# Last layer of a two-layer decoder: values and context table in one PSUM bank, three norms on ScalarE, a new order of the turn

## The chip, the cores and the metric

One core of a Trainium2 chip. The metric is the device time of one launch in microseconds (us). Engines are named as in the profile: PE (TensorE, matmul), DVE (VectorE), ACT (ScalarE), POOL (GpSimd), SP (SyncE, here only a DMA queue). SBUF is the working memory of 128 partitions, PSUM the eight banks that PE writes its results to; POOL reads and writes SBUF alone.

## What is computed

The reference applies six blocks to x of shape (2, 1024, 256), each as `x = layernorm(x + block(x))` with eps 1e-5 and no gain or bias. Layer 0 has a causal linear attention, a cross attention with quantised weights and a mixture of eight experts of which each token takes one. Layer 1, the last, is the part that the change is about:

```python
def attn1(x):                          # per token, 16 heads of 16
    Q, K, V = (heads(x @ W.T) for W in (W_Q, W_K, W_V))
    sK = softmax(swapaxes(K, -1, -2))          # softmax over the 16 numbers of each head of K
    tran_V = einsum('bldh,blhe->blde', sK, V)  # a 16 x 16 table for every token
    return einsum('blhd,blde->blhe', softmax(Q), tran_V)

def xattn1(x, ctx):                    # 16 heads of 64, 64 context rows in one frame
    xn = layernorm(x) * gamma + beta
    return softmax(q @ k.T * 64**-0.5 + mask) @ v @ Wo + bo

def ffn1(x):                           # 256 -> 1024 -> 1024 -> 1024 -> 256, ternary weights
    h = silu((x @ w1.T) * s1) * ((x @ w2.T) * s2)
    h = gelu((h @ h1.T) * sh1); h = gelu((h @ h2.T) * sh2)
    return (h @ w3.T) * s3

x = layernorm(x + attn1(x)); x = layernorm(x + xattn1(x, ctx)); x = layernorm(x + ffn1(x))
```

## The kernel before

The program runs its stages one after the other, each with its own instruction list per engine and semaphores between them. Two stages matter here.

**Experts** (`stage_experts`, L1457 on). 23 slots of 128 rows go through two matmul layers. SP's queue loads a slot's rows (`rows`, L1497, 128 KB) and its expert's first weights (`weights`, L1491, 1024 KB) into one of two buffers, `following` (L1501) waits until the buffer is free and loads both. Rows and weights of the first two slots are loaded by the stage before. At its start the queue waits for the copy of the last layer's weights to be complete, issues three loads for later (`wqkv1` of 768 KB, `w1` and a piece of 1024 KB each, L1508 to L1511), and then `following(2, 0)`. On PE, `turn_rows` (L1537) turns a slot's rows and `hidden` (L1544) and `output` do the matmuls; the third slot's rows are turned between the hidden layers of the first and the second.

**The last layer** (`stage_layer1`, L1685 on). Tokens are 16 tiles of 128, eight blocks i of both sequences b (k = 2i + b counts them). A tile has a long chain through the engines: moments of x (DVE), a power -0.5 (POOL, `power`), the normed x3 (DVE, L2205), its turning (PE, `turned_x3`) and copy (ACT, `x3_copied`), the projection (PE, `qkv`), softmaxes of Q and K (DVE and ACT), the 16 x 16 tables (`contexts`) and their product with Q (`attended`), the norm x4 and beside it xn for the cross attention (DVE, L2264), scores (PE), their maximum (DVE), 16 exponentials with sums (ACT, `score_exp`), probabilities (DVE), their turning (PE), `summed` (PE), the norm x5. Then both tiles of a block, a pair j of 256 tokens, go through the feed-forward part: `first` (eight units of two products), two `hidden` layers (eight units of 16 matmuls each) and `final`. All its operands are split in a high and a low part: ACT writes the high part, POOL subtracts for the low one (`gate_lower`, `lower_parts`).

DVE does the per-token tables by hand: `contexts` and `attended` (L2234, L2244) come in four quarters, each of two products of 128x512 and two reduces after them, written as

```python
products(..., lambda at, n: V.tensor_tensor(part[n], spread(kn[:, at:at + TWO, :], 2, DH),
                                            spread(vs[b][:, :, :], 1, TWO), ALU.mult),
         lambda at, n: V.tensor_reduce(to[:, at:at + TWO, :], part[n], AX.X, ALU.add))
```

The values `vs[b]` are an SBUF tile (it shares its place with `xT[b]`), filled from PSUM bank 3 by an ACT copy (`v_copied`, L2064). The table `T` is an SBUF tile too. The other half of bank 3 takes the turned x3.

The order of the work is written out by hand, once per engine, in a function `trip(n)` (L1831 POOL, L2004 PE, L2128 ACT, L2338 DVE): the trip of turn n does the start of block n, the attentions of block n - 1, the feed-forward part of block n - 2 and the last norm of block n - 3. `tile`, `pair` and `row_of` leave out what lies outside the eight blocks. A turn here is the time from one first `final` to the next. Each engine runs its list strictly in order, so an instruction that waits holds everything behind it; no planner moves anything.

Before the first trip, POOL issues 16 gathers of the experts' results (L1864 to L1872) with the first two `x_powered` between them, after the sixth and the twelfth gather. After the last `final`, the last norm `y_normed` (DVE, L2333) and a store of 128 KB per tile end the program.

## Time and profile before

| | us |
|---|---|
| median of 3 runs (1346.11 to 1347.29) | 1346.78 |
| the profiled execution, whole | 1346.4 |
| its span on the core | 1344.8 |
| PE busy in the span | 1073.1 (80%) |
| DVE busy | 936.4 (70%) |
| ACT busy | 591.8 (44%) |
| POOL busy | 359.6 (27%) |

Busy is the time in which an engine executes an instruction; waiting in a queue is not in it. The span runs from the first to the last instruction. The last layer takes a little over half of it, from 636 us to the end. The mean granted clock of PE over the span is 0.917 of full speed.

### The profile page before, as it was taken

The numbers are of one execution on the slowest core, as the hardware profiler recorded it, in microseconds if no ns is written. First come the engines' busy times: TensorE is split into PE (matmuls) and PEld (weight loads), VectorE is DVE, ScalarE is ACT, GpSimd is POOL, SyncE is SP. The second block draws the span as 40 slices with busy tenths as digits, with TensorE's granted clock in tenths as the row PEclk, the third lists the DMA queues.
The fourth block names the chain that finished last, engine by engine and source line by source line (L and its number), as shares of the span: only waits on it lengthen the run. The fifth ranks groups of instructions, "written<-read, shape, count | busy, mean of one in ns | idle before, by whom it ended". The sixth has DMA issues, their size and how long they took to land. (4 is left out here: it accounts for less than half of the span.)

```text
span 1344.8 us, 21004 instructions
## 1 busy us (share of the span) xinstructions
PE 1073.1 (80%) x6765; PEld 895.6 (67%) x6770; DVE 936.4 (70%) x1861; ACT 591.8 (44%) x1626; POOL 359.6 (27%) x494
## 2 busy tenths in 40 slices
PE   0589999766888599998344798889888898897887
PEld 0478888644366488887122687677767787786787
DVE  4689999765774022222599998989898998989231
ACT  0244444141263232232022556567566656747552
POOL 1001011100034200000400435436262633536232
PEclk9889999885896799999667799999999999999899
DMA  8015710002402566664440000000000000000000
GB/s 286 19 71 184 237 49 5 0 1 109 174 1 94 197 226 226 242 222 153 172 203 1 1 1 1 8 0 8 0 4 4 0 8 0 8 0 9 1 9 9
DMA packets 24263, 98.88 MB, mean 74 GB/s; under 512 B 3761, under 2 KB 15217, under 8 KB 17617
## 3 DMA queue, kind: packets, MB, share of 16 engines
q1 hardware_dynamic: 16368, 73.60, 14.8%
q10 hardware_dynamic: 5200, 17.37, 3.9%
q0 software_dynamic: 2640, 7.21, 1.6%
q8 instruction: 30, 0.49, 0.2%
q14 instruction: 25, 0.20, 0.1%
HBM read 87.96 MB, written 21.76 MB: 82 GB/s over the span
## 5 line engine op out<-in xcount | busy, mean ns | idle before, releaser
L1989 PE MATMUL bank<-n_hA_hi_reduced,ffn_h 128*128 128x256 f32 x512 | 126.8, 290 | 9.2 <-POOL n_hA_lo_reduced L1812 5.5
L1989 PE MATMUL bank<-n_hB_hi_reduced,ffn_h 128*128 128x256 f32 x512 | 129.9, 296 | 1.5 <-DVE n_hB_lo_reduced L2326 1.5
L1989 PE MATMUL bank<-n_hB_lo_reduced,ffn_h 128*128 128x256 f32 x512 | 125.4, 287 | 0.0
L1989 PE MATMUL bank<-n_hA_lo_reduced,ffn_h 128*128 128x256 f32 x512 | 123.8, 284 | 0.0
L1606 ACT ACTIVATE e_hT<-bank,e_b 128x128 f32<-128x128 f32 x184 | 52.4, 368 | 135.4 <-PE bank L1549 135.4
L1989 PEld LDWEIGHTS bank<-n_hA_hi_reduced,ffn_h 128*128 128x128 f32 x512 | 99.2, 194 | 11.0 <-POOL n_hA_lo_reduced L1812 10.2
L1989 PEld LDWEIGHTS bank<-n_hB_hi_reduced,ffn_h 128*128 128x128 f32 x512 | 101.1, 197 | 3.3 <-issue 3.3
L2240 DVE TENSOR_TENSOR d_prod<-d_qk,d_xT 128x512 f32<-128x512 f32 x128 | 102.6, 841 | 0.5
L1989 PEld LDWEIGHTS bank<-n_hB_lo_reduced,ffn_h 128*128 128x128 f32 x512 | 101.0, 197 | 1.7 <-issue 1.7
L1989 PEld LDWEIGHTS bank<-n_hA_lo_reduced,ffn_h 128*128 128x128 f32 x512 | 99.1, 194 | 0.2
L1631 DVE TENSOR_TENSOR e_y<-bank,e_b 128x256 f32<-128x256 f32 x23 | 9.8, 424 | 125.3 <-PE bank L1561 125.3
L2252 DVE TENSOR_TENSOR d_prod<-d_qk,d_T 128x512 f32<-128x512 f32 x128 | 92.4, 761 | 0.3
L1549 PE MATMUL bank<-e_xsT,e_w 128*128 128x128 f32 x736 | 88.3, 279 | 0.2 <-DVE e_xsT L1623 0.2
L1819 POOL TENSOR_TENSOR n_hA_lo_reduced<-n_hA_lo,n_hA_hi_reduced 128x256 fp32r<-128x256 f32 x60 | 55.3, 922 | 123.9 <-ACT n_hA_lo L2125 123.3
L1549 PEld LDWEIGHTS bank<-e_xsT,e_w 128*128 128x128 f32 x736 | 86.5, 196 | 0.6 <-DVE e_xsT L1623 0.6
L1561 PE MATMUL bank<-w2e,e_hT 128*128 x368 | 83.1, 379 | 0.0
L2242 DVE TENSOR_REDUCE d_T<-d_prod 128x32 f32<-128x512 f32 x128 | 81.2, 674 | 0.0
L2254 DVE TENSOR_REDUCE d_r<-d_prod 128x32 f32<-128x512 f32 x128 | 81.1, 673 | 0.0
L562 PE MATMUL bank<-a_prod_a,ident 128*128 128x160 f32 x512 | 75.5, 307 | 7.0 <-DVE a_prod_a L714 6.1
L1970 PE MATMUL bank<-d_x5T_hi_reduced,ffn_w 128*128 128x256 f32 x256 | 66.1, 298 | 16.7 <-ACT n_hB_lo L2105 9.1
L562 PEld LDWEIGHTS bank<-a_prod_a,ident 128*128 128x128 f32 x512 | 71.8, 194 | 10.8 <-DVE a_prod_a L714 10.7
L2084 ACT ACTIVATE d_pr<-bank,d_score_max 128x64 f32<-128x64 f32 x256 | 75.9, 349 | 2.2 <-DVE d_score_max L2277 2.0
(344 smaller groups left out, 2686.1 us busy)
## 6 DMA issues: line engine op xcount, KB each, us to landing
e_w<-in_W SPq DMA_DIRECT2D x23, 1024.0 KB, 5.2
ffn_weights<-in_F ACTq DMA_DIRECT2D x2, 5632.0 KB, 20.8
e_piece<-ffn_weights SPq DMA_DIRECT2D x11, 1024.0 KB, 4.8
ffn_h<-ffn_weights SPq DMA_DIRECT2D x2, 4096.0 KB, 18.8
w2e<-in_W SPq DMA_DIRECT2D x1, 4096.0 KB, 13.2
w2e<-in_W SPq DMA_DIRECT2D x2, 2048.0 KB, 16.6
ffn_w<-ffn_weights SPq DMA_DIRECT2D x3, 1024.0 KB, 7.4
expert_rows<-zero ACTq DMA_DIRECT2D x1, 2944.0 KB, 10.7
```

The source lines that it names most:

```text
L562: last = nc.tensor.matmul(bank_a[:, 0:PAIRS], m.ident[:, :], prod_a[:, d, :], start=(d == 0), stop=(d == DH - 1))
L1549: last = nc.tensor.matmul(bank_h[u][f // 4][:, f % 4 * P:(f % 4 + 1) * P], w1[u][:, k, f * P:(f + 1) * P], xsT[u][:, k, :], start=(k == 0) ...
L1561: last = nc.tensor.matmul(bank_y[u][:, 0:D], hT[u][:, k, :], m.w2e[:, bass.ds(e, 1), k, :], start=(k == 0), stop=(k == KF - 1))
L1606: last = nc.scalar.activation(hT[u][:, k, :], bank_h[u][k // 4][:, k % 4 * P:(k % 4 + 1) * P], ACT.Relu, bias=b1[:, bass.ds(e, 1), k])
L1819: nc.gpsimd.tensor_tensor(dst[1][1][:, f, :], dst[1][0][:, f, :], dst[0][1][:, f, :].bitcast(F32), ALU.subtract).then_inc(ready, 1)
L1970: last = nc.tensor.matmul(F[f % 2][:, n * PAIR:(n + 1) * PAIR], weight(w[:, k, f * P:(f + 1) * P], fast), operand(x5T[part][1][:, k, :, :] ...
L1989: last = nc.tensor.matmul(F[f % 2][:, 0:PAIR], weight(w[:, k, f * P:(f + 1) * P], fast), operand(src[part][1][:, k, :], fast), start=(c == ...
L2084: last = nc.scalar.activation(pr[:, h * SC:(h + 1) * SC], bank_s[h // 8][:, h % 8 * SC:(h % 8 + 1) * SC], ACT.Exp, bias=score_max[b][:, 1, ...
L2240: lambda at, n: V.tensor_tensor(part[n], spread(kn[:, at:at + TWO, :], 2, DH), spread(vs[b][:, :, :], 1, TWO), ALU.mult),
L2242: lambda at, n: V.tensor_reduce(to[:, at:at + TWO, :], part[n], AX.X, ALU.add))
L2252: lambda at, n: V.tensor_tensor(part[n], spread(qn[:, at:at + TWO, :], 2, DH), spread(T, 1, TWO), ALU.mult),
L2254: lambda at, n: V.tensor_reduce(heads[:, at:at + TWO, :], part[n], AX.X, ALU.add))
```

## The change

- **Bank.** `T` and the values become the two halves of bank 3, read by DVE where PE wrote them. `vs`, the ACT copies `v_copied` and the SBUF table go. The projection of the values is split from `qkv` into `projected_v` with a place of its own in PE's list; it waits for `v_read`, which DVE signals after the last quarter of `attended`. The turned x3 goes to the second half of bank 4.
- **Norms.** x3, x4 and the last norm are computed by ACT as rstd * x + (-mean * rstd) in one instruction; POOL makes the offset with two more products on [128x1] after its power. xn stays on DVE. `out_summed` on DVE now waits for x4 from ACT.
- **Order.** All four lists are reordered; ACT's last norms need a trip more at the end. POOL's first two `x_powered` come after four and eight gathers.
- **Experts.** The third rows' load is issued ahead of the three later loads, on `xs_turned` alone.

```diff
+sp.wait_ge(xs_turned, 1)
+rows(2, 0)
 sp.wait_ge(m.weights_copied, 32)
 sp.dma_start(m.wqkv1[:, :, :], ins["wqkv1"]).then_inc(m.early_loaded, 16)
 sp.dma_start(m.w1[:, :, :].rearrange("p k n -> p (k n)"), m.ffn[:, 0:2 * FF]).then_inc(m.early_loaded, 16)
 sp.dma_start(piece[:, :], m.ffn[:, 0:2 * FF]).then_inc(piece_loaded, 16)
-following(2, 0)
+sp.wait_ge(h_done, 2)
+weights(2, 0)
...
-vs = [t[:, :, :].rearrange("p k (e h) -> p (k e) h", h=H) for t in xT]
-T = late("d_T", [P, DH, DH], F32)[:, :, :]
...
+T = bank_v[:, D:2 * D].rearrange("p (e d) -> p e d", e=DH)
+values = bank_v[:, 0:D].rearrange("p (e h) -> p e h", h=H)
...
+def negated(st, to):
...
+    return nc.gpsimd.tensor_tensor(st[:, to:to + 1], st[:, 6:7], m.mhalf[:, 2:3], ALU.mult)
...
+def offset(st, rstd, to):
...
+    return nc.gpsimd.tensor_tensor(st[:, to:to + 1], st[:, to:to + 1], st[:, rstd:rstd + 1], ALU.mult)
...
 def attn_powered(k, i, b):
     g.wait_ge(q["attn_var"], k + 1)
-    nc.gpsimd.tensor_tensor(stats[b][:, 10:12], stats[b][:, 8:10], m.mhalf[:, :],
+    after("x4", k - 1)
+    nc.gpsimd.tensor_tensor(stats[b][:, 10:12], stats[b][:, 8:10], m.mhalf[:, 0:2],
                             ALU.pow).then_inc(q["attn_pow"], 1)
+    negated(stats[b], 12).then_inc(q["x4_less"], 1)
+    g.wait_ge(q["attn_pow"], k + 1)
+    g.wait_ge(q["x4_less"], k + 1)
+    offset(stats[b], 10, 12).then_inc(q["x4_offset"], 1)
...
 def x_powered(k, i, b):
     powered(k, "x", xstats[b])
+    after("x3", k - 1)
+    negated(xstats[b], 10).then_inc(q["x_less"], 1)
+    g.wait_ge(q["x_pow"], k + 1)
+    g.wait_ge(q["x_less"], k + 1)
+    offset(xstats[b], 9, 10).then_inc(q["x_offset"], 1)
...
 def y_powered(j, b):
     g.wait_ge(y_var, 2 * j + b + 1)
     power(nc, m, ystats[b]).then_inc(y_pow, 1)
+    negated(ystats[b], 10).then_inc(y_less, 1)
+    g.wait_ge(y_pow, 2 * j + b + 1)
+    g.wait_ge(y_less, 2 * j + b + 1)
+    offset(ystats[b], 9, 10).then_inc(y_offset, 1)
...
 def trip(n):
     if not (isinstance(n, int) and n < 2):
         tile(x_powered, n, 0)
+    pair(lower_parts, n - 3, 1, 4, 8)
+    tile(out_powered, n - 2, 1)
     tile(attn_powered, n - 1, 0)
     if isinstance(n, int) and n == 1:
         x_powered(2, 1, 0)
-    pair(gated_product, n - 2, 0, 2)
+    tile(x5_kept, n - 2, 1)
+    row_of(added, n - 3, 0)
+    row_of(added, n - 3, 1)
+    pair(gated_product, n - 2, 0, 4)
     pair(gate_lower, n - 2, 0, 1)
-    pair(gated_product, n - 2, 2, 4)
-    pair(gate_lower, n - 2, 1, 2)
-    pair(gated_product, n - 2, 4, 5)
-    pair(gate_lower, n - 2, 2, 3)
-    pair(gated_product, n - 2, 5, 8)
+    pair(gated_product, n - 2, 4, 6)
+    pair(gate_lower, n - 2, 1, 3)
+    pair(gated_product, n - 2, 6, 8)
     pair(gate_lower, n - 2, 3, 8)
-    row_of(added, n - 3, 1)
     row_of(y_powered, n - 3, 0)
-    pair(lower_parts, n - 2, 0, 0, 2)
     row_of(y_powered, n - 3, 1)
-    pair(lower_parts, n - 2, 0, 2, 5)
-    tile(attn_powered, n - 1, 1)
     if not (isinstance(n, int) and n == 0):
         tile(x_powered, n, 1)
-    pair(lower_parts, n - 2, 0, 5, 8)
+    pair(lower_parts, n - 2, 0, 0, 6)
+    tile(attn_powered, n - 1, 1)
+    pair(lower_parts, n - 2, 0, 6, 8)
     tile(out_powered, n - 1, 0)
+    pair(lower_parts, n - 2, 1, 0, 2)
     tile(x5_kept, n - 1, 0)
-    pair(lower_parts, n - 2, 1, 0, 8)
-    tile(out_powered, n - 1, 1)
-    tile(x5_kept, n - 1, 1)
-    row_of(added, n - 2, 0)
+    pair(lower_parts, n - 2, 1, 2, 4)
...
     g.wait_ge(m.y_stored[u], 16 * ((NS + 1 - u) // 2))
 for t in range(TB):
-    if t == 3:
+    if t == 2:
         x_powered(0, 0, 0)
-    elif t == 6:
+    elif t == 4:
         x_powered(1, 0, 1)
...
 def turned_x3(k, i, b):
     pe.wait_ge(q["x3"], k + 1)
-    after("v_copied", k)
+    after("x3T", k)
+    after("out_var", k - 2)
     for c in range(KD):
-        last = nc.tensor.transpose(bank_v[:, D + c * P:D + (c + 1) * P], x3[b][:, c * P:(c + 1) * P],
+        last = nc.tensor.transpose(bank_o[:, D + c * P:D + (c + 1) * P], x3[b][:, c * P:(c + 1) * P],
                                    m.ident[:, :])
     last.then_inc(q["x3_turned"], 1)
...
 def qkv(k, i, b):
     pe.wait_ge(q["x3T"], k + 1)
     after("pre", k)
-    for lo, hi, to in ((0, 2 * D, bank_qk), (2 * D, 3 * D, bank_v)):
-        for c in range(KD):
-            last = nc.tensor.matmul(to[:, 0:hi - lo], xT[b][:, c, :], m.wqkv1[:, c, lo:hi],
-                                    start=(c == 0), stop=(c == KD - 1))
+    for c in range(KD):
+        last = nc.tensor.matmul(bank_qk[:, 0:2 * D], xT[b][:, c, :], m.wqkv1[:, c, 0:2 * D],
+                                start=(c == 0), stop=(c == KD - 1))
     last.then_inc(q["qkv_done"], 1)
+def projected_v(k, i, b):
+    pe.wait_ge(q["x3T"], k + 1)
+    after("v_read", k)
+    for c in range(KD):
+        last = nc.tensor.matmul(bank_v[:, 0:D], xT[b][:, c, :], m.wqkv1[:, c, 2 * D:3 * D],
+                                start=(c == 0), stop=(c == KD - 1))
+    last.then_inc(q["v_done"], 1)
...
 def summed(k, i, b):
     pe.wait_ge(q["probT"], k + 1)
     after("out_var", k)
+    pe.wait_ge(q["x3T"], min(k + 3, NT) if isinstance(k, int) else k + 3)
...
@@ -2007,25 +2046,30 @@
     tile(qkv, n, 0)
     pair(hidden, n - 2, 0, 0, 2, fast)
     tile(turned_probs, n - 1, 0)
-    pair(hidden, n - 2, 0, 2, 7, fast)
+    pair(hidden, n - 2, 0, 2, 6, fast)
     tile(summed, n - 1, 0)
+    pair(hidden, n - 2, 0, 6, 7, fast)
+    tile(projected_v, n, 0)
     tile(turned_xn, n - 1, 1)
     pair(hidden, n - 2, 0, 7, 8, fast)
+    tile(scores, n - 1, 1)
+    pair(hidden, n - 2, 1, 0, 1, fast)
     tile(turned_x3, n, 1)
-    tile(scores, n - 1, 1)
-    pair(hidden, n - 2, 1, 0, 3, fast)
+    pair(hidden, n - 2, 1, 1, 2, fast)
+    tile(qkv, n, 1)
+    pair(hidden, n - 2, 1, 2, 4, fast)
     tile(turned_x5, n - 1, 0)
-    pair(hidden, n - 2, 1, 3, 5, fast)
-    tile(qkv, n, 1)
     tile(turned_probs, n - 1, 1)
-    pair(hidden, n - 2, 1, 5, 8, fast)
+    pair(hidden, n - 2, 1, 4, 8, fast)
     tile(summed, n - 1, 1)
     row_of(final, n - 2, 0, fast)
+    tile(turned_x5, n - 1, 1)
     row_of(final, n - 2, 1, fast)
-    tile(turned_x5, n - 1, 1)
-    pair(first, n - 1, 0, 4, fast)
+    pair(first, n - 1, 0, 1, fast)
+    tile(projected_v, n, 1)
+    pair(first, n - 1, 1, 2, fast)
     tile(turned_xn, n, 0)
-    pair(first, n - 1, 4, 8, fast)
+    pair(first, n - 1, 2, 8, fast)
     tile(scores, n, 0)
...
-def v_copied(k, i, b):
-    act.wait_ge(q["qkv_done"], k + 1)
-    nc.scalar.activation(vs[b][:, :, :].rearrange("p a b -> p (a b)"), bank_v[:, 0:D],
-                         ACT.Copy).then_inc(q["v_copied"], 1)
...
 def xn_copied(k, i, b):
     act.wait_ge(q["xn_turned"], k + 1)
+    act.wait_ge(q["v_done"], k + 1)
...
+def x3_normed(k, i, b):
+    act.wait_ge(q["x_offset"], k + 1)
+    after("xn_turned", k - 1)
+    nc.scalar.activation(x3[b][:, :].unsqueeze(1), m.x[:, row(i, b), :], ACT.Identity,
+                         bias=xstats[b][:, 10:11], scale=xstats[b][:, 9:10]).then_inc(q["x3"], 1)
+def x4_normed(k, i, b):
+    act.wait_ge(q["x4_offset"], k + 1)
+    after("out_var", k - 1)
+    nc.scalar.activation(x4[b][:, :], r[b][:, :], ACT.Identity, bias=stats[b][:, 12:13],
+                         scale=stats[b][:, 10:11]).then_inc(q["x4"], 1)
+def y_normed(j, b):
+    act.wait_ge(y_offset, 2 * j + b + 1)
+    nc.scalar.activation(m.x[:, row(j, b), :], m.x[:, row(j, b), :], ACT.Identity,
+                         bias=ystats[b][:, 10:11], scale=ystats[b][:, 9:10]).then_inc(y_ready, 1)
 def trip(n):
+    tile(x3_normed, n, 0)
+    pair(gate_upper, n - 2, 5, 6)
     tile(x3_copied, n, 0)
-    pair(gate_upper, n - 2, 7, 8)
+    pair(gate_upper, n - 2, 6, 8)
     tile(score_exp, n - 1, 0)
-    pair(hidden, n - 2, 0, 0, 5)
+    pair(hidden, n - 2, 0, 0, 1)
+    row_of(y_normed, n - 3, 0)
+    row_of(y_normed, n - 3, 1)
+    pair(hidden, n - 2, 0, 1, 2)
     tile(probs_copied, n - 1, 0)
-    pair(hidden, n - 2, 0, 5, 7)
+    pair(hidden, n - 2, 0, 2, 4)
+    tile(x4_normed, n - 1, 0)
+    pair(hidden, n - 2, 0, 4, 6)
     tile(qk_exp, n, 0)
+    tile(x3_normed, n, 1)
     tile(xn_copied, n - 1, 1)
-    pair(hidden, n - 2, 0, 7, 8)
-    tile(v_copied, n, 0)
+    pair(hidden, n - 2, 0, 6, 8)
     pair(hidden, n - 2, 1, 0, 1)
     tile(x3_copied, n, 1)
-    pair(hidden, n - 2, 1, 1, 3)
+    pair(hidden, n - 2, 1, 1, 2)
     tile(score_exp, n - 1, 1)
-    pair(hidden, n - 2, 1, 3, 4)
+    pair(hidden, n - 2, 1, 2, 4)
     tile(x5_copied, n - 1, 0)
-    tile(v_copied, n, 1)
-    pair(hidden, n - 2, 1, 4, 6)
     tile(probs_copied, n - 1, 1)
-    pair(hidden, n - 2, 1, 6, 8)
+    tile(x4_normed, n - 1, 1)
+    pair(hidden, n - 2, 1, 4, 8)
+    tile(qk_exp, n, 1)
     tile(x5_copied, n - 1, 1)
-    tile(qk_exp, n, 1)
-    pair(first, n - 1, 0, 2)
+    pair(first, n - 1, 0, 4)
     pair(gate_upper, n - 1, 0, 1)
-    pair(first, n - 1, 2, 4)
-    pair(gate_upper, n - 1, 1, 2)
     pair(first, n - 1, 4, 6)
     tile(xn_copied, n, 0)
-    pair(gate_upper, n - 1, 2, 4)
+    pair(gate_upper, n - 1, 1, 4)
     pair(first, n - 1, 6, 8)
-    pair(gate_upper, n - 1, 4, 7)
-for n in range(2):
+    pair(gate_upper, n - 1, 4, 5)
+for n in range(3):
     trip(n)
-with act.Fori(0, TB - 2) as i:
-    trip(i + 2)
-for n in range(TB, TB + 2):
+with act.Fori(0, TB - 3) as i:
+    trip(i + 3)
+for n in range(TB, TB + 3):
...
-def x3_normed(k, i, b):
-    v.wait_ge(q["x_pow"], k + 1)
-    after("xn_turned", k - 1)
-    V.tensor_scalar(x3[b][:, :].unsqueeze(1), m.x[:, row(i, b), :], xstats[b][:, 6:7],
-                    xstats[b][:, 9:10], ALU.subtract, ALU.mult).then_inc(q["x3"], 1)
...
-    v.wait_ge(q["v_copied"], k + 1)
+    v.wait_ge(q["v_done"], k + 1)
...
              lambda at, n: V.tensor_tensor(part[n], spread(kn[:, at:at + TWO, :], 2, DH),
-                                           spread(vs[b][:, :, :], 1, TWO), ALU.mult),
+                                           spread(values, 1, TWO), ALU.mult),
...
+    if quarter == 3:
+        v.sem_inc(q["v_read"], 1)
...
-    link(V.tensor_scalar(x4[b][:, :], r[b][:, :], stats[b][:, 6:7], stats[b][:, 10:11], ALU.subtract,
-                         ALU.mult))
...
 def out_summed(k, i, b):
     v.wait_ge(q["out_done"], k + 1)
+    v.wait_ge(q["x4"], k + 1)
     link(V.tensor_tensor(r[b][:, :], bank_o[:, 0:D], x4[b][:, :], ALU.add))
...
-def y_normed(j, b):
-    v.wait_ge(y_pow, 2 * j + b + 1)
-    V.tensor_scalar(m.x[:, row(j, b), :], m.x[:, row(j, b), :], ystats[b][:, 6:7], ystats[b][:, 9:10],
-                    ALU.subtract, ALU.mult).then_inc(y_ready, 1)
...
 def trip(n):
     if not (isinstance(n, int) and n == 1):
         tile(x3_moments, n, 0)
-    tile(x3_normed, n - 1, 1)
+    tile(softmaxes, n - 1, 0)
+    tile(x4_and_xn, n - 2, 1)
+    tile(contexts, n - 1, 0, 0)
     tile(out_summed, n - 2, 0)
-    tile(softmaxes, n - 1, 0)
-    tile(contexts, n - 1, 0, 0)
-    tile(x5_normed, n - 2, 0)
+    tile(contexts, n - 1, 0, 1)
     tile(scores_max, n - 2, 1)
-    tile(contexts, n - 1, 0, 1)
     tile(contexts, n - 1, 0, 2)
     tile(contexts, n - 1, 0, 3)
+    tile(x5_normed, n - 2, 0)
+    tile(prepared, n - 1, 1)
     tile(probabilities, n - 2, 1)
     tile(attended, n - 1, 0, 0)
     tile(attended, n - 1, 0, 1)
-    tile(x5_split, n - 2, 0)
     tile(attended, n - 1, 0, 2)
     tile(attended, n - 1, 0, 3)
     tile(out_summed, n - 2, 1)
-    tile(prepared, n - 1, 1)
+    tile(x5_split, n - 2, 0)
     tile(x5_normed, n - 2, 1)
     if isinstance(n, int) and n == LAST + 3:
         last_lower_parts(0)
         last_lower_parts(1)
     row_of(sums_read, n - 3, 0)
+    tile(attention_summed, n - 1, 0)
+    tile(x5_split, n - 2, 1)
     row_of(sums_read, n - 3, 1)
-    tile(x5_split, n - 2, 1)
     if isinstance(n, int) and n == LAST + 2:
         last_gates()
-    tile(attention_summed, n - 1, 0)
-    row_of(y_moments, n - 3, 0)
     tile(softmaxes, n - 1, 1)
     tile(x4_and_xn, n - 1, 0)
     if isinstance(n, int) and n == 1:
         x3_moments(2, 1, 0)
+    row_of(y_moments, n - 3, 0)
     tile(contexts, n - 1, 1, 0)
+    row_of(y_moments, n - 3, 1)
     tile(contexts, n - 1, 1, 1)
     tile(contexts, n - 1, 1, 2)
-    tile(x3_normed, n, 0)
     tile(scores_max, n - 1, 0)
     tile(contexts, n - 1, 1, 3)
     tile(attended, n - 1, 1, 0)
+    tile(x3_moments, n, 1)
     tile(probabilities, n - 1, 0)
-    row_of(y_moments, n - 3, 1)
-    row_of(y_normed, n - 3, 0)
     tile(attended, n - 1, 1, 1)
-    row_of(y_normed, n - 3, 1)
     tile(attended, n - 1, 1, 2)
-    tile(x3_moments, n, 1)
+    tile(prepared, n, 0)
     tile(attended, n - 1, 1, 3)
     tile(attention_summed, n - 1, 1)
-    tile(prepared, n, 0)
-    tile(x4_and_xn, n - 1, 1)
...
-TRIP_LINKS = 108
+TRIP_LINKS = 106
```

(Twelve spaces of indentation are left out.) `TRIP_LINKS` counts the waits of DVE on itself in a trip.

## Rows read from the trace of the kernel before

**Rows 1.** Busy time by stage: from:to, length, PE, PEld, DVE, ACT, POOL, granted clock, DMA.

```profile
635.90:821.70 185.80, 112.44 (x530) 81.81 (x531) 156.62 (x296) 65.82 (x227) 54.79 (x65) 0.78 0.18 69
...
821.70:897.60 75.90, 65.99 (x449) 56.57 (x448) 68.95 (x128) 48.84 (x144) 35.98 (x44) 1.00 0.01 4
...
897.60:975.50 77.90, 67.94 (x451) 58.33 (x449) 71.00 (x130) 48.77 (x144) 35.63 (x44) 0.98 0.01 3
...
1207.20:1282.60 75.40, 63.54 (x430) 57.25 (x429) 44.06 (x83) 44.53 (x137) 33.20 (x42) 0.93 0.01 4
```

**Rows 2.** Groups of PE, five turns: busy us, mean ns, idle before by releaser.

```profile
L1928 PE MATMUL bank<-ident,d_pr 128*128 128x128 f32 x80 | 11.3, 285 | 16.4 <-DVE d_pr L2284 16.4
...
L1891 PE MATMUL bank<-ident,d_x 128*128 128x128 f32 x20 | 4.2, 294 | 14.2 <-ACT d_xT L2066 7.9 <-DVE d_x L2208 6.3
```

**Rows 3.** Groups of DVE over the same five turns, 821.7 to 1207.2 us.

```profile
L2240 DVE TENSOR_TENSOR d_prod<-d_qk,d_xT 128x512 f32<-128x512 f32 x80 | 66.3, 869 | 0.3
...
L2252 DVE TENSOR_TENSOR d_prod<-d_qk,d_T 128x512 f32<-128x512 f32 x80 | 59.4, 781 | 0.2
...
L2268 DVE TENSOR_SCALAR d_x<-d_r,d_stats 128x256 f32<-128x256 f32 x10 | 8.2, 819 | 0.0
...
L2214 DVE TENSOR_TENSOR d_qk<-bank,d_mx 128x512 f32<-128x512 f32 x10 | 6.9, 691 | 0.3
...
L2213 DVE TENSOR_REDUCE d_mx<-bank 128x32 f32<-128x512 f32 x10 | 6.8, 680 | 0.0
...
L2220 DVE TENSOR_REDUCE d_mx<-d_qk 128x32 f32<-128x512 f32 x10 | 6.8, 680 | 0.0
...
L2335 DVE TENSOR_SCALAR x_tok<-x_tok,d_ystats x10 | 6.2, 616 | 0.0
...
L2208 DVE TENSOR_SCALAR d_x<-x_tok,d_xstats 128x256 f32 (+1 forms) x10 | 4.0, 405 | 1.0 <-issue 0.7 <-DVE d_x L2268 0.3
...
L2283 DVE RECIPROCAL d_score_sum<-d_score_sum 128x16 f32<-128x16 f32 x10 | 2.5, 253 | 16.0 <-ACT d_pr L2084 15.3
```

**Rows 4.** Timeline of DVE in the fill: start us, us, instruction.

```profile
663.81 1.27 DVE L2240 TENSOR_TENSOR d_prod<-d_qk,d_xT 128x512 f32<-128x512 f32 x2
...
673.48 1.28 DVE L2252 TENSOR_TENSOR d_prod<-d_qk,d_T 128x512 f32<-128x512 f32 x2
```

**Rows 5.** Timeline of PE in a turn.

```profile
992.83 1.88 PE L1921 MATMUL bank<-cross_M,d_xT 128*128 128x512 f32 x4
...
1048.18 3.62 PE L1936 MATMUL bank<-cross_N,d_pT 128*128 128x256 f32 x16
```

**Rows 6.** Timeline of ACT in a turn.

```profile
997.19 1.28 ACT L2084 ACT_TABLE_LOAD   x1
...
1003.34 1.28 ACT L2123 ACT_TABLE_LOAD   x1
...
1009.90 0.47 ACT L2123 ACTIVATE n_hB_hi_reduced<-bank,sc 128x256 fp32r<-128x256 f32 x1 [1.05 <-PE bank L1989]
...
1011.78 0.47 ACT L2123 ACTIVATE n_hB_hi_reduced<-bank,sc 128x256 fp32r<-128x256 f32 x1 [1.04 <-PE bank L1989]
```

**Rows 7.** Group of POOL, five turns.

```profile
L466 POOL TENSOR_TENSOR d_xstats<-d_xstats,mhalf 128x1 f32<-128x1 f32 x10 | 5.7, 567 | 0.1
```

**Rows 8.** Timeline of POOL before the first trip.

```profile
646.62 0.94 POOL L1871 DMA_INDIRECT g_rows<-expert_out,slot  x1 [0.30 <-issue]
...
647.58 0.60 POOL L466 TENSOR_TENSOR d_xstats<-d_xstats,mhalf 128x1 f32<-128x1 f32 x1
```

**Rows 9.** Experts: timeline of SP's queue and PE; DMA issues, KB, median us to landing.

```profile
450.83 0.89 SPq L1499 DMA_DIRECT2D e_xs<-expert_rows  x1
...
450.80 4.87 PE L1549 MATMUL bank<-e_xsT,e_w 128*128 128x128 f32 x32 [0.17 <-DVE e_xsT L1623]
...
460.10 0.69 PE L1540 MATMUL bank<-ident,e_xs 128*128 128x128 f32 x2 [4.43 <-DMA e_xs<-expert_rows]
...
e_xs<-expert_rows SPq DMA_DIRECT2D x23, 128.0 KB, 4.5
```

More of the change, by code:

```diff
@@ L191, in constants @@
                                      base=0, pattern=[[-1, 4], [1, n]], channel_multiplier=0))
[L192 removed]
+    link(nc.gpsimd.memset(m.mhalf[:, 0:2], -0.5))
+    link(nc.gpsimd.memset(m.mhalf[:, 2:4], -1.0))
     link(nc.gpsimd.memset(m.rep[:, :], 1.0))
@@ L1782, in _, with after @@
         def _(g):
+            def after(name, count):
+                if not (isinstance(count, int) and count <= 0):
+                    g.wait_ge(q[name], count)
             def powered(k, name, st):
```

11 lines of the change are left out of this document (5 added, 6 removed).

## The prediction

> **What bounds the kernel now.** Read the busy time by stage first. The last layer runs in turns, one per token block and both sequences; in the middle a turn takes 75.9 us, or 77.9 us where TensorE's granted clock dipped (0.98 over that turn) [rows 1]. PE is busy 66 to 68 us of it, DVE 69 to 71, ACT 49, POOL 36: two engines near full, neither full. So the next views are the groups of PE and of DVE over five turns, and what ended the idle time before them. PE loses 16.4 us in five turns waiting for the probabilities from DVE and 14.2 before the turning of x3 [rows 2]; with the smaller waits, before `first` above all, 9.6 us a turn. DVE's one large wait is 16.0 us in five turns for ACT's exponentials [rows 3]; with the small ones it idles 4.9 us a turn, so it is occupied for 71.0. DVE is the engine that ends most waits, and PE follows it.
>
> The third view says why DVE is that full. A pair of products takes 1.27 to 1.28 us where POOL is quiet [rows 4], 0.64 each. Over the five turns, with POOL at work, the same instructions take 66.3/80 = 0.83 and 59.4/80 = 0.74 us of busy time [rows 3]. The reduces between them aren't stretched. What sets the products apart is that they read two SBUF operands. L2214, as long, reads one operand from a PSUM bank and one from SBUF; half of its ten runs lie under POOL's work, and its mean is 691 ns [rows 3], which is what each of them takes.
>
> **The change, part by part.**
>
> *Values and table in a bank.* Each turn has 16 products of either kind. With one operand in the bank they should cost 0.64 as L2214 suggests: (0.83-0.64)x16 + (0.74-0.64)x16 = 4.6 us of DVE per turn. Two ACT copies go. No row shows DVE writing a bank (the 16 reduces of the contexts will). Bounds: a product from a bank could cost what L2214 has over the quiet pair, 0.69-0.64 = 0.05 more, or by the same amount less; I take 0, since a lone instruction shows its whole latency and in a pair the next one covers a part of it.
>
> The Trainium skill speaks against this: "VectorE: DVE Perf Modes", the section on the TRN2 errata, gives a fixed 58 cycles for an SBUF source and 120 for a PSUM source, by its clock an estimate of 65 ns more per instruction. With that on all 64 products and reduces my sum would be 1327 instead. This trace doesn't show it: L2213 and L2220, the same reduce of 512 elements from a bank and from SBUF, have 680 ns both [rows 3].
>
> *New wait.* Values and table share one bank with one buffer, so PE's projection of the next values waits for `v_read`, at the end of the last product. Queued behind it on PE are the turning of xn, scores and the hidden units. Laid out in order, PE arrives 5 us (tile 0) and 8 us (tile 1) after that signal; DVE then waits up to 1.3 us for `v_done`.
>
> *Three norms to ACT.* DVE loses L2268 (8.2/5 = 1.64 us a turn), L2335 (1.24) and L2208 (0.80) [rows 3]: 3.7 us. ACT gains six instructions of at most the 0.47 us of a Gelu of this size [rows 6]: 2.8 us on 49 of 76, beside other work. POOL gains two [128x1] products per norm, 12 a turn. No row shows such a product; the power of the same shape takes 0.57 [rows 7], and the other end is nothing. I take 0.55: +6.6 us on 36, hidden in steady turns, but 1.1 us longer from variance to norm. Where it isn't hidden is the end: the last two rows go pow, negate, offset, twice, on one queue, +2.0 us (0 if the product is free, and then 2.4 us less in all).
>
> *DVE after.* 71.0 - 4.6 - 3.7 = 62.7 us. That is 10 under the new turn, so DVE stops being the bound, and the gain is set by what is late next.
>
> *The new turn.* I set the four queues beside each other in their new order with these durations and followed what ends last. The loop that closes:
> 1. PE turns the second tile's probabilities (0.9), four units of the second hidden layer (1.88 each, from two ACT starts [rows 6]), `summed` (3.6 [rows 5]): 12.0.
> 2. DVE sum and moments 1.3, POOL power 0.6, DVE x5 0.5: 2.4.
> 3. PE turns x5 and does the second `final`: 2.3.
> 4. DVE reads the sum, the softmax scaling, xn: 3.2.
> 5. PE turns xn, six units of `first` (half of 1.88 each) with 2 us of waits on ACT, scores (two halves of 1.9 [rows 5]), x3: 10.4.
> 6. ACT copies x3, two gate copies, table load and 16 exponentials (997.19 to 1003.34 [rows 6], 6.15): 7.1.
> 7. DVE probabilities 1.6.
> 8. PE: probabilities 0.9, six units 11.3, `summed` 3.3, values 0.9, xn 0.2, scores 3.8, two units 3.8, x3 0.3: 24.5.
> 9. ACT: two Gelus, then 6.15: 6.9.
> 10. DVE probabilities 1.6.
> Sum 72.0; with the small gaps 72.2. The same walk over the old order gives 75.8 where the clock-steady turns show 75.9, so I trust the difference, 3.6, more than either. What remains of PE's waits is mainly steps 6, 7, 9 and 10, 5.4 us a turn: more than the 3.3 it waits for probabilities now, while the waits at x3 and at `first` nearly go.
> Five intervals at 3.6 make 18.0. The next, with half the DVE work (75.4 [rows 1]), goes from 72.3 to 70.3 in the walk: 2.0. The last two have no attention left: 0.
>
> *The fill.* 185.8 us from the layer's start to the first `final` [rows 1], DVE-bound. The first power moves from behind six gathers to behind four, 2.5 us earlier (the sixth starts at 646.62, the power at 647.58 [rows 8]), less 1.2 for the two added products: 1.3; the first projection without the values, at the low clock, 0.8. The four x3 and three x4 norms up to there: 2.6 of DVE. Up to 752 POOL is quiet and no product is stretched; the last 70 us run beside POOL like a turn, 0.92 of its 4.6 us, and 0.7 of stretched norms: 4.9. Together 9.6; new waits (the scores of the third turn, `v_done`) give back 2.0. I take 7.6, between 3 and 10.
>
> *Experts.* The third rows' load is issued at 450.83 behind three transfers of 768 to 1024 KB on SP's queue, and PE waits 4.43 us for it [rows 9]. Sent first at 450.2, when the first rows have been turned, even at the median of its kind, 4.5 us, it lands at 454.7, before PE is free at 455.7 [rows 9]. All 4.43 go there. But the weights of expert 2 and the fourth rows still queue behind the 2.8 MB, which took some 10 us, and PE now asks for them that much sooner: I estimate 0.8 given back. 3.6 (2 to 4.4); other stages shift by it.
>
> *Sum.* -7.6 - 18.0 - 2.0 + 2.0 + 0.2 (rounding of the last intervals) - 3.6 = -29.0 from the profiled execution's 1346.4: 1317.4. The median of the runs is 0.4 above it: 1317.8. A memset more among the constants and the reordered POOL queue hide beside DVE.
>
> **The rivals.**
>
> *The lock stays* (the change doesn't do what it says). If it is the write into SBUF that collides, or any instruction of two operands, a bank operand doesn't free the products. For it: POOL's own instructions stretch too. Against: ten runs of L2214 at one duration. The norms still go; the walk gives a turn of 73.6 and 15.8 in all: 1346.8 - 15.8 - 3.6 = 1327.4.
>
> *The bank is dearer.* 0.05 us on each of the 64 instructions a turn: 3.2 us of DVE, hidden in the turn (72.5), but not in the DVE-bound fill, where it costs 5 to 6. Gain 18.4 + 3.6: 1324.8. The skill's estimate above lies 2 us beyond.
>
> *The new order gives the turn's gain back.* The path crosses engines nine times a turn, and any product of ACT that comes late at the two score steps is waited for by PE. For it: PE's wait for probabilities grows. Against: the walk of the old order is right to 0.1 us. With the turn at 75.8: only fill, experts and end remain, -7.6 - 3.6 + 2.0: 1337.6.
>
> *Slower.* One place: the 16 strided reduces that write the table into the bank, and the products that read it back. If writing and re-reading cost 0.2 us more on each of the 64, DVE has 62.7 + 12.8 = 75.5 of work plus its waits: turn 76.6, fill 198, end +21.2 - 3.6 = 1364. It decides from 0.15, where the walk is at 692.7 us for the layer against 692.3 before. Against: no bank row is over 0.05 dearer; for: no row writes one.
>
> **How the numbers follow.** Forecast 0.60, own range 1307 to 1328 (turns between 71 and 74, fill and experts at their bounds); lock stays 0.10; bank dearer 0.08; gain given back 0.10; slower 0.08; 0.04 unnamed, half no change, half slower. The range 1303 to 1337 takes in the first three and part of the fourth; below it lies a turn under 70.5, hardly above PE's own 66. Less than 0.2% (2.7 us) can't be told from no change here. Faster: 0.60 + 0.10 + 0.08 + 0.09 = 0.87; same 0.02 + 0.01, and 0.01 of the slower case: 0.04; slower 0.09.
>
> **What would show it.** L2240's and L2252's successors at 0.64 per product with POOL busy (right), or at 0.8 (lock stays), or at 0.7 everywhere (bank dearer). DVE busy some 61 to 63 us a turn and no longer the one that others wait for; PE's wait before L1928's successor at 4 to 6 us a turn, those at x3 and `first` under 1. Turns of 72 to 73.5 us between `final`s. No wait before the third turning of expert rows, at most 1 us before the fourth. The last norm some 2 us further behind the last variance. The forecast is wrong if turns stay over 75 or if PE stalls at the values' projection.

## The result, and the profile after

The changed kernel takes 1336.7 us (median of four runs, 1335.8 to 1336.9) against 1346.4 for the kernel before (1345.0 to 1347.3): ratio 0.9941, 95% interval 0.9923 to 0.9959. It is 0.6% faster, by 9.7 us and not by the 29 of the forecast. The profiled spans, 1344.8 and 1335.3, differ by 9.5, and that can be laid out by stretch. The first turning of expert rows on PE, PE's last transpose of the experts, the first sum of gathered rows on DVE and the first `final` of each block mark the borders; the fourth column is the best experiment (e9, below), put here for comparison.

| us | before | changed | e9 | forecast of the change |
|---|---|---|---|---|
| start to the first turning of expert rows | 449.6 | 451.0 | 451.2 | 0 |
| experts | 185.8 | 181.8 | 180.3 | -3.6 |
| to the layer's first sum of rows | 7.7 | 8.4 | 8.5 | 0 |
| first stage, to the first `final` | 178.6 | 177.7 | 170.9 | -7.6 |
| five turns | 385.4 | 381.1 | 364.4 | -18.0 |
| next interval | 75.5 | 73.2 | 71.6 | -2.0 |
| the interval after it, the last between first `final`s | 52.7 | 52.0 | 51.2 | 0 |
| from the last block's first `final` to the end | 9.4 | 10.2 | 10.2 | +2.0 |

The experts and the next interval went about as forecast, and the end cost less. The first stage and the turns did not: 5.2 us came of 25.6. The view by stage shows what became of them (columns as in [rows 1]); first the first stage of the kernel before, then the changed kernel:

```profile
643.10:821.72 178.62, 112.46 (x531) 81.83 (x531) 156.38 (x294) 65.82 (x227) 52.40 (x62) 0.79 0.18 70
```

```profile
641.12:818.83 177.71, 112.02 (x526) 83.01 (x527) 148.42 (x285) 71.19 (x233) 50.98 (x85) 0.78 0.18 70
...
818.83:894.47 75.64, 68.55 (x451) 59.53 (x449) 61.53 (x122) 51.10 (x148) 32.90 (x56) 0.95 0.01 4
894.47:971.25 76.78, 69.68 (x450) 60.60 (x449) 61.58 (x122) 51.11 (x148) 32.86 (x56) 0.93 0.01 3
...
1199.96:1273.11 73.15, 64.24 (x434) 57.48 (x433) 36.92 (x77) 44.27 (x139) 30.30 (x50) 0.95 0.01 5
```

DVE fell from 69 to 71 us a turn to 61.5, as forecast. But PE rose from 66.0 in a turn at full clock [rows 1] to 68.6 and 69.7 with the same number of instructions, and the granted clock, 1.00 in that turn before, is 0.95 and 0.93. The groups over the same five turns, PE's first (columns as in [rows 2]):

```profile
L1966 PE MATMUL bank<-ident,d_pr 128*128 128x128 f32 x80 | 17.6, 393 | 27.6 <-DVE d_pr L2339 27.6
...
L1922 PE MATMUL bank<-ident,d_x 128*128 128x128 f32 x20 | 3.8, 272 | 0.0
```

```profile
L2297 DVE TENSOR_REDUCE bank<-d_prod 128x32 f32<-128x512 f32 x80 | 51.2, 685 | 0.0
L2307 DVE TENSOR_TENSOR d_prod<-d_qk,bank 128x512 f32<-128x512 f32 x80 | 51.1, 680 | 0.2
L2295 DVE TENSOR_TENSOR d_prod<-d_qk,bank 128x512 f32<-128x512 f32 x80 | 51.0, 679 | 5.1 <-PE bank L1938 5.1
...
L2344 DVE TENSOR_TENSOR d_r<-bank,d_x 128x256 f32<-128x256 f32 x10 | 4.2, 420 | 20.9 <-PE bank L1975 20.9
```

PE's wait at x3 [rows 2] is gone. That for the probabilities went from 16.4 to 27.6 us, and the transposes behind it from 285 to 393 ns each: they run slowly. DVE, the second fence, has its products at 51.0/80 = 0.64 us of busy time (66.3/80 and 59.4/80 in [rows 3]), and now waits 4.2 us a turn for PE (L2344). The timeline of PE shows the two waits of a turn and the slow matmuls behind the first (start us, us, instruction, what it waited for), and the view by stage the two stretches behind the two waits, with the clock in the third column from the end:

```profile
922.38 1.97 PE L1966 MATMUL bank<-ident,d_pr 128*128 128x128 f32 x8 [2.62 <-DVE d_pr L2339]
...
924.36 0.41 PE L2028 MATMUL bank<-n_hA_lo_reduced,ffn_h 128*128 128x256 f32 x1
924.57 0.41 PE L2028 MATMUL bank<-n_hA_hi_reduced,ffn_h 128*128 128x256 f32 x1
...
925.42 0.28 PE L2028 MATMUL bank<-n_hA_hi_reduced,ffn_h 128*128 128x256 f32 x1
925.54 0.28 PE L2028 MATMUL bank<-n_hA_lo_reduced,ffn_h 128*128 128x256 f32 x1
...
956.94 1.97 PE L1966 MATMUL bank<-ident,d_pr 128*128 128x128 f32 x8 [2.93 <-DVE d_pr L2339]
```

```profile
922.30:925.70 3.40, 3.32 (x17) 3.33 (x18) 3.40 (x7) 3.32 (x8) 1.73 (x4) 0.54 0.23 77
...
956.90:963.10 6.20, 6.16 (x30) 6.17 (x31) 6.20 (x11) 3.92 (x10) 2.31 (x5) 0.51 0.00 0
```

After the wait of 2.62 PE runs at 1.2 GHz for some 3 us, matmuls 0.21 apart, and then at 2.4 again, 0.12 apart; after that of 2.93 for some 6. All ten long waits of the five turns (2.50 to 2.94 us) have such a stretch, which starts between 0.9 us before the end of the wait and 1.4 us after it. Behind the second wait it is the longer kind in two turns, those of 76.8 and 77.1; all the others are some 3 us long. In the kernel before, the wait of 2.12 in front of the second transposes had one in three turns of five, the three of 77.8 to 77.9; one of these had a second, behind a wait of 1.29 in front of the transposes of x3.

### The profile page after: what moved, and what is told of

It is laid out like the page before. It is cut to its first block and busy times, and to the rows that moved or that the text cites. A ratio compares the mean times of both kernels' runs of the same rounds, so it can differ in the third digit from the quotient of the medians.

```text
span 1335.3 us, 21219 instructions
## 1 busy us (share of the span) xinstructions
PE 1084.4 (81%) x6769; PEld 909.5 (68%) x6770; DVE 878.3 (66%) x1813; ACT 610.7 (46%) x1658; POOL 342.0 (26%) x591
## 5 line engine op out<-in xcount | busy, mean ns | idle before, releaser
L2028 PE MATMUL bank<-n_hA_hi_reduced,ffn_h 128*128 128x256 f32 x512 | 132.7, 299 | 5.8 <-DVE n_hA_lo_reduced L2375 3.5
L2028 PE MATMUL bank<-n_hB_hi_reduced,ffn_h 128*128 128x256 f32 x512 | 134.1, 303 | 1.5 <-DVE n_hB_lo_reduced L2382 1.5
L2028 PE MATMUL bank<-n_hA_lo_reduced,ffn_h 128*128 128x256 f32 x512 | 128.4, 291 | 0.0
L2028 PEld LDWEIGHTS bank<-n_hA_hi_reduced,ffn_h 128*128 128x128 f32 x512 | 103.9, 203 | 11.0 <-POOL n_hA_lo_reduced L1839 10.6
L2028 PEld LDWEIGHTS bank<-n_hA_lo_reduced,ffn_h 128*128 128x128 f32 x512 | 103.6, 202 | 0.2
L2295 DVE TENSOR_TENSOR d_prod<-d_qk,bank 128x512 f32<-128x512 f32 x128 | 81.7, 679 | 7.8 <-PE bank L1938 7.7
L2297 DVE TENSOR_REDUCE bank<-d_prod 128x32 f32<-128x512 f32 x128 | 81.9, 685 | 0.0
L2307 DVE TENSOR_TENSOR d_prod<-d_qk,bank 128x512 f32<-128x512 f32 x128 | 81.7, 680 | 0.3
L563 PE MATMUL bank<-a_prod_a,ident 128*128 128x160 f32 x512 | 75.8, 307 | 7.1 <-DVE a_prod_a L715 6.2
L1846 POOL TENSOR_TENSOR n_hA_lo_reduced<-n_hA_lo,n_hA_hi_reduced 128x256 fp32r<-128x256 f32 x60 | 44.0, 733 | 130.5 <-ACT n_hA_lo L2165 130.5
L1565 PEld LDWEIGHTS bank<-w2e,e_hT 128*128 128x128 f32 x368 | 68.2, 190 | 8.4
## 6 DMA issues: line engine op xcount, KB each, us to landing
expert_rows<-zero ACTq DMA_DIRECT2D x1, 2944.0 KB, 10.6
```

Of the source, the lines that this page charges most:

```text
L563: last = nc.tensor.matmul(bank_a[:, 0:PAIRS], m.ident[:, :], prod_a[:, d, :], start=(d == 0), stop=(d == DH - 1))
L1565: last = nc.tensor.matmul(bank_y[u][:, 0:D], hT[u][:, k, :], m.w2e[:, bass.ds(e, 1), k, :], start=(k == 0), stop=(k == KF - 1))
L1846: nc.gpsimd.tensor_tensor(dst[1][1][:, f, :], dst[1][0][:, f, :], dst[0][1][:, f, :].bitcast(F32), ALU.subtract).then_inc(ready, 1)
L2028: last = nc.tensor.matmul(F[f % 2][:, 0:PAIR], weight(w[:, k, f * P:(f + 1) * P], fast), operand(src[part][1][:, k, :], fast), start=(c == ...
L2307: lambda at, n: V.tensor_tensor(part[n], spread(qn[:, at:at + TWO, :], 2, DH), spread(T, 1, TWO), ALU.mult),
```

## The experiments

Theory A: these stretches took the gain; the forecast timetable is right at full clock. Theory B, the prediction's third rival: the new order itself closes the turn at 75.8. To tell them apart PE gets something to do while it waits, matmuls whose results nobody reads (`warm`), into a bank that nobody else uses at that time. Ratios below are to the kernel before on the same chip (medians 1343.2 beside e1 to e4, 1346.4 beside e5 to e8, 1342.0 beside e9 to e11, 1346.1 beside e12 and e13); the changed kernel's is 0.9941.

**Both waits filled (e1), one filled (e3), the waits alone (e7), the kernel before filled (e2).**

```diff
+            def warm(count):
+                for _ in range(count):
+                    nc.tensor.matmul(bank_o[:, 0:D], m.identb[:, :],
+                                     m.maskb[:, 0:1, :].broadcast_to([P, D // SC, SC]), start=True, stop=True)
             def turned_probs(k, i, b):
+                after("out_var", k)
+                pe.wait_ge(q["x3T"], min(k + 3, NT) ...)
+                warm(16)        # e3: for b == 1 only; e7: none; e2: 12, in the kernel before
                 pe.wait_ge(q["prob"], k + 1)
```

> The changed kernel with 16 more matmuls (128x128 by 128x256, results never read) put on PE in front of each transpose of the probabilities, where PE waits 2.6 and 2.9 us a turn. Theory A (the clock took the gain: after each of these two waits the trace shows PE's matmuls 0.21 us apart instead of 0.115 for 3 to 6 us): the waits fall under 1.2 us, no slow stretch follows, turns fall from 75.6 to 77.1 to 72 to 73.2, the interval before the last pairs by 1 to 2, the whole to 1313 to 1321 us. Theory B (the new order itself closes the turn at 75.8, through DVE and ACT): turns stay at 75.5 to 77, the whole within 2 us of 1336.7, or over it by what the added matmuls hold up.

Measured: 1315.25 us, ratio 0.9783 (0.9758 to 0.9809). Turns of 72.5 to 73.0. By stage, and by groups of PE over five turns:

```profile
816.95:889.49 72.54, 68.93 (x482) 59.39 (x481) 61.51 (x122) 50.83 (x148) 32.98 (x56) 1.00 0.01 4
889.49:962.42 72.93, 69.36 (x482) 59.84 (x481) 61.51 (x122) 50.86 (x148) 32.91 (x56) 1.00 0.01 4
```

```profile
L1966 PE MATMUL bank<-maskb,identb 128*128 128x256 bf16 x160 | 19.2, 273 | 0.0
L1975 PE MATMUL bank<-ident,d_pr 128*128 128x128 f32 x80 | 10.9, 279 | 10.0 <-DVE d_pr L2348 10.0
```

The clock holds at 1.00 in the turns. PE's own work is 69.4 - 19.2/5 = 65.6 us a turn where the changed kernel needs 68.6 to 70.0; what PE doesn't work (waits and added matmuls together, 7.3) is what the changed kernel waits (7.1). The time without real work hardly shrank; filled, it stopped costing the clock. Theory A holds, B falls.

> The changed kernel with the 16 matmuls in front of the second transpose of a turn only (the wait of 2.9 us). Theory A: only the stretch after the first wait stays slow; turns 73.5 to 75, the whole 1323 to 1330, between the changed kernel and the one with both filled. Theory B: within 2 us of 1336.7.

Measured: 1319.6 us, ratio 0.9824 (0.9805 to 0.9844): better than theory A asked (1323 to 1330). Turns alternate:

```profile
815.25:887.81 72.56, 67.20 (x467) 57.90 (x465) 61.59 (x122) 50.83 (x148) 33.00 (x56) 1.00 0.01 4
887.81:962.20 74.39, 69.03 (x467) 59.78 (x465) 61.52 (x122) 50.98 (x148) 32.90 (x56) 0.98 0.01 4
```

A slow stretch costs 1.8 to 1.9 us a turn where it comes; with the second wait filled the first one, 2.5 us in every turn, is followed by one in only two of the five.

> e1_fill_both without the added matmuls: only its two waits ahead of the transposes of the probabilities, which are met long before. If the matmuls made the gain (theory A): the slow stretches are back, turns 75.6 to 77, the whole within 2 us of the changed kernel, 1333 to 1338 where before is 1343 to 1346. If the place of the waits made it: 1315 as e1_fill_both.

Measured: 1337.55 us, ratio 0.9936 (0.9908 to 0.9964); turns 75.7 to 77.2, clock 0.95 and 0.93 as in the changed kernel. One of the turns, beside the 72.93 of e1:

```profile
896.14:973.02 76.88, 69.73 (x450) 60.73 (x449) 61.51 (x122) 51.01 (x148) 32.87 (x56) 0.93 0.01 3
```

The matmuls made the gain, not the waits' place.

> The kernel before the change with 12 such matmuls in front of each transpose of the probabilities (waits of 1.46 and 2.12 us). Theory A: the slow stretches that three of five turns have after the wait of 2.12 go, all turns at 75.9 (DVE holds them there), the whole 5 to 8 us less, 1338 to 1342. Theory B: 1346 within 1.5 us.

Measured: 1339.41 us, ratio 0.9966 (0.9950 to 0.9981). Turns 75.9 to 76.7, where before had three of 77.8 to 77.9: theory A's sign, a little under its size (3.8 us). Two turns, of 76.7 and 76.6, still dip (0.98), now behind waits of 1.3 us in front of the transposes of x3, which were not filled.

**The first stage and the last turns (e5, e9).** As e1, with `warm` also in PE's second turn and, in e9, ahead of the last turns' waits:

```diff
+                if isinstance(n, int) and n == 1:
+                    warm(40, bank_s[0])          # e9: 72
                 tile(turned_xn, n - 1, 1)
...
+                    pe.wait_ge(q["out_var"], 1)
+                    warm(20)                     # e9: 36
                 tile(turned_x5, n - 1, 0)
...
```

and in the same way 8 ahead of `summed`, 16 and 6 (e9: 50 and 6) ahead of the second `turned_x5` and of `first`; e9 adds 8 ahead of `scores`, 14 and 26 ahead of the hidden units of the last two trips, and has 32 instead of 16 ahead of the last probabilities.

> As e1_fill_both, and in the layer's first stage too (second turn of PE's list only): added matmuls in front of the transposes of xn (40) and of x5 (20 and 16), the sums (8) and the first FFN layer (6), where PE waits 9.1, 4.2, 2.7, 1.2 and 1.1 us. Theory A (in the first stage too it is the clock that ate the gain: it is at half from 703.8 to 714, 720.9 to 731, 738 to 751.7 and 755 to 761.8, and DVE then waits 2.1, 1.6 and 4.5 us for PE): these waits of DVE shrink by 4 to 6 us in all, the first final comes 4 to 7 us sooner after the layer's start, the whole 4 to 7 us under e1_fill_both (1308 to 1311 beside 1315). Theory C (the first stage is held by DVE's and ACT's own steps): within 1.5 us of e1_fill_both, or over it where the added matmuls hold up real ones.

Measured: 1316.0 us, ratio 0.9781 (0.9749 to 0.9813): no gain over e1. A miss for theory A as put, but not a test: the matmuls ran out 5.3 and 4.5 us before the waits ended, and the half clock was back. (The times of half clock that the expectation names lie 10.5 us after those of the changed kernel's profile, where they run from 693.3 to 703.5, 710.4 to 720.6, 727.4 to 741.1 and 744.5 to 751.3.)

> e5_fill_start with the matmuls of the first stage made long enough for its waits (72, 36, 8, 50, 6, and 8 in front of the scores; in e5 PE was idle for 5.3 and 4.5 us after 40 and 16 of them and the slow stretches came back), and 14, 26 and 32 in front of the waits of 2.2, 3.5 and 3.0 us in the last turns. Theory A: DVE's waits for PE in the first stage (2.1 to 3.2, 1.0 to 1.6 and 4.0 to 4.6 us) fall by 3 to 5 us in all, the first final comes 170 to 172 us after the layer's first sum of rows instead of 174.7, the last turns gain 1 to 3: 1309 to 1313 where e1_fill_both is 1315. If the first stage is not held by the clock: 174 to 175 and the whole at 1313 to 1316.

Measured: 1308.55 us, ratio 0.9741 (0.9700 to 0.9781), the lowest median of this study. Its interval overlaps e1's; what it adds to e1 is read from the stages, of one profiled execution each:

```profile
640.00:810.87 170.87, 130.84 (x771) 99.86 (x771) 148.31 (x285) 70.86 (x233) 51.09 (x84) 0.86 0.19 73
810.87:883.83 72.96, 69.50 (x483) 59.95 (x481) 61.53 (x122) 50.80 (x148) 32.90 (x56) 1.00 0.01 4
...
1175.29:1246.90 71.61, 67.92 (x497) 60.34 (x495) 36.86 (x77) 44.10 (x139) 30.35 (x50) 1.00 0.01 5
```

The first stage takes 170.9 (178.6 before, 174.7 in e1), with the clock at 1.00 in every later stretch up to the last `final`; e1, e6 and e13, which fill the turns alike, and e5 have 174.2 to 174.9. So there too the clock had eaten the gain: DVE's work is the changed kernel's (148.3 and 148.4 us), and its idle time falls from 29.3 to 22.6.

**What each part is worth at full clock (e4, e6, e10, e11, e12, e13), and the rows alone (e8).** The table alone goes back to SBUF in e4 (changed kernel) and e6 (e1); values and table both, with ScalarE's copy of the values, in e11 (changed kernel), e10 and e12 (with the fill); e13 puts the three norms back on VectorE in e1.

```diff
-    T = bank_v[:, D:2 * D].rearrange("p (e d) -> p e d", e=DH)
+    T = late("d_T", [P, DH, DH], F32)[:, :, :]                                # e4, e6, e10 to e12
-    values = bank_v[:, 0:D].rearrange("p (e h) -> p e h", h=H)
+    vs = [t[:, :, :].rearrange("p k (e h) -> p (k e) h", h=H) for t in xT]    # e10 to e12
 e12, against e10:
+                tile(ahead, n - 1, 0)            # the two waits and warm(14)
                 pair(hidden, n - 2, 0, 0, 2, fast)
 and in turned_probs warm(16) for b == 1 only
 e13, against e1: on VectorE again, for x3, x4 and y
+                V.tensor_scalar(x3[b][:, :].unsqueeze(1), m.x[:, row(i, b), :], xstats[b][:, 6:7],
+                                xstats[b][:, 9:10], ALU.subtract, ALU.mult).then_inc(q["x3"], 1)
 e8, against the kernel before:
+            sp.wait_ge(xs_turned, 1)
+            rows(2, 0)
             sp.wait_ge(m.weights_copied, 32)
...
-            following(2, 0)
+            sp.wait_ge(h_done, 2)
+            weights(2, 0)
```

> The changed kernel with the context table back in SBUF (the values stay in the bank): the 16 second products of a turn read two SBUF operands again. Theory A (PE and its clock hold the turn, DVE has 14 us of waits): the products go from 0.68 to 0.72 to 0.80, DVE is busy 1 to 2 us more a turn, and the turn gains at most 1: 1336 to 1343. Theory B' (DVE still holds the turn): all of it comes through, 1.5 to 2 us a turn, 1345 to 1349. The reduces that write the table stay at 0.68 if writing the bank costs nothing.

> e1_fill_both with the context table back in SBUF (its products took 0.725 there, 0.68 in the bank, 16 a turn: 0.7 us). If, with the clock held, DVE or the chain from scores to probabilities sets the turn: turns 0.3 to 0.8 longer than the 72.9 of e1_fill_both, the whole 2 to 5 us over it (1317 to 1320 beside 1315). If the turn is PE's and DVE's waits take it up: within 1 us.

Measured: e4 1334.2, ratio 0.9941 (0.9924 to 0.9958), as the changed kernel; e6 1315.0, ratio 0.9767 (0.9727 to 0.9807), as e1. DVE's groups in e4:

```profile
L2307 DVE TENSOR_TENSOR d_prod<-d_qk,d_T 128x512 f32<-128x512 f32 x80 | 54.8, 725 | 0.2
...
L2297 DVE TENSOR_REDUCE d_T<-d_prod 128x32 f32<-128x512 f32 x80 | 50.9, 678 | 0.0
```

The second products are 45 ns longer, their place doesn't move the time, and a reduce into SBUF takes 678 ns against 685 into the bank.

> The changed kernel with values and context table both back in SBUF, without added matmuls: what the bank alone is worth under the slow clock. If it is covered there (DVE has 14 us of waits a turn in the changed kernel): within 3 us of the changed kernel, 1334 to 1340. If the forecast's step of 4.6 us of DVE a turn still counts: turns 1 to 3 us longer, 1340 to 1352.

Measured: 1331.35, ratio 0.9931 (0.9909 to 0.9952): without the added matmuls the bank is worth nothing in the whole. That is not its price alone, since the slow stretches came less often: two turns escaped them and took 73.1 and 73.3; two that didn't took 76.8 and 77.0:

```profile
817.62:894.58 76.96, 70.40 (x451) 61.22 (x449) 65.44 (x122) 51.75 (x150) 38.32 (x56) 0.93 0.01 4
894.58:967.70 73.12, 65.65 (x450) 56.27 (x449) 64.91 (x122) 51.60 (x150) 38.82 (x56) 1.00 0.01 4
```

> e1_fill_both with values and context table both back in SBUF (values copied by ScalarE as before the change): all 32 products of a turn read two SBUF operands. By the rows of the kernel before they take 0.73 to 0.87 instead of 0.68, 16 x 0.05 + 16 x 0.15 = 3 us more DVE a turn. If DVE or its chain sets the turn now: turns at 74 to 76, the whole 6 to 15 us over e1_fill_both. If not (DVE has 5 to 9 us of waits a turn there): turns within 1 us of 72.9, the whole 0 to 5 us over.

Measured: 1328.7, ratio 0.9904 (0.9879 to 0.9929), turns 73.8 to 75.6. Not a clean price: here the first wait was gone and the added matmuls held PE up. Hence e12, with them where PE now waited.

> e10_fill_no_bank with the first group of added matmuls moved: in e10 the 16 in front of the first transpose of the probabilities held PE up (the wait there was gone, 995.7 against 994.5), and PE's 1.9 us wait stood two FFN blocks earlier, for POOL. Now 14 stand there. What the bank is worth with the clock held: the forecast (4.6 us of DVE a turn, of which most comes through) wants turns 2 to 4 us longer than the 72.9 of e1_fill_both, 75 to 77; if the turn is not DVE's, 73 to 73.8 (the two turns of e11_no_bank without a slow stretch took 73.1 and 73.3), the whole 1315 to 1320.

Measured: 1325.75, ratio 0.9858 (0.9810 to 0.9906), turns 73.6 to 74.2. DVE's groups:

```profile
L2320 DVE TENSOR_TENSOR d_prod<-d_qk,d_xT 128x512 f32<-128x512 f32 x80 | 66.7, 872 | 10.5 <-ACT d_xT L2127 10.5
L2332 DVE TENSOR_TENSOR d_prod<-d_qk,d_T 128x512 f32<-128x512 f32 x79 | 53.3, 713 | 0.2
```

With the clock held in the turns the bank is worth 1.0 us a turn (73.9 - 72.9), and in the first stage 4.5 by e12 (179.2 from the first sum of rows to the first `final`, 174.7 in e1) or 2.5 by e10 (177.3); 0.75% in all by the ratios, give or take 0.5. It is the place of the values that counts, since the table's alone (e6) gives nothing. Whether their operand does it (15.7 us more of DVE in five turns) or ScalarE's copy, for which DVE now waits 10.5 us where e1 waits 5.1 for the projection, no run tells apart.

> e1_fill_both with the three norms back on VectorE (bank, order, rows and added matmuls kept): DVE gets 6 instructions of 0.40 to 0.62 a turn again, some 3.0 to 3.7 us occupied, ScalarE and POOL lose theirs. If DVE's occupation sets the turn: turns 2 to 4 us longer, 75 to 77, the whole 1327 to 1338. If order and PE set it: within 1 us a turn, 1313 to 1320.

Measured: 1316.3, ratio 0.9788 (0.9751 to 0.9826); turns 72.8 to 73.2, DVE at 64.1 us, the clock 1.00. With the clock held, moving the norms off DVE is worth nothing that shows.

> The kernel before with the experts' third rows loaded sooner and nothing else. The forecast's step: the wait of 4.43 before the third turning of rows goes and 0.8 comes back, 3.6 us less from the experts' first turning to the layer's start (before: 449.55 to 635.36, 185.8), the rest unchanged: the whole 3 to 4.5 us less. If the changed kernel's shorter experts came from elsewhere: 0.

Measured: 1341.2, ratio 0.9966 (0.9949 to 0.9983), 4.6 us with 2.3 either way. The wait before the third turning is gone; the fourth turning now waits. In e8:

```profile
457.52 0.38 PE L1543 MATMUL bank<-ident,e_xs 128*128 128x128 f32 x2
...
467.54 0.44 PE L1543 MATMUL bank<-ident,e_xs 128*128 128x128 f32 x2 [2.61 <-DMA e_xs<-expert_rows]
```

In the changed kernel, the same two:

```profile
456.91 0.38 PE L1544 MATMUL bank<-ident,e_xs 128*128 128x128 f32 x2
...
466.15 0.44 PE L1544 MATMUL bank<-ident,e_xs 128*128 128x128 f32 x2 [1.83 <-DMA e_xs<-expert_rows]
```

## Why the prediction was wrong

**The step that failed** is "The new turn": the loop summed to 72.0, "with the small gaps 72.2", from PE durations at full clock. It ended with PE waiting "5.4 us a turn" for probabilities, more than before, and left PE's durations as they were. Two of its items were longer on the chip. Item 1 (12.0, from the second probabilities to the `final`) took 12.8 to 14.3 in the five turns, 13.5 on average; item 8 (24.5, from the first probabilities to the end of its two units) 25.8 to 26.1. In the turn shown above they run from 956.94 to the `final` at 971.25 and from 922.38 to 948.14. Both begin behind the long waits. In e1 the same two take 11.7 and 24.5: the walk had them right at full clock, and the 3.3 us between are the difference of the turns, 76.2 on average and 72.9. "I trust the difference, 3.6" was the error: the walk over the old order was checked against the turn whose clock had held, and the turn of 77.9 beside it [rows 1], slow behind its longest wait, 2.12 us, was set aside. That row was the warning; the new order made its wait longer and added a second one. What the forecast said of the waits themselves came true: 27.6/5 = 5.5 us a turn for probabilities. (Item 5's prices add to 11.9 and not to its 10.4; 10.6 was measured, so the slip did no harm.)

That e1 has the forecast's ratio (0.978) is partly luck. Its five turns gave 21.0 and not 18.0, because the old turns, 77.1 on average, were not the clean 75.9 of the forecast, and its first stage gave 3.9 and not 7.6.

**The fill** (7.6): 0.9 came. DVE's work fell by 8.0 us (156.4 to 148.4), about as forecast; the term that failed is the new waits, "give back 2.0". DVE's idle time in the stage rose from 22.2 to 29.3, so they gave back 7.1. With the clock held from 704 us on (e9) it is 22.6, and 7.8 came. Not all single waits are the clock's: the longest, 4.52 us before the third turn's scores, is still 4.04 in e9, where PE runs the eight units of `first` ahead of these scores; those that e9 loses are 2.1 before the second turn's scores, 1.6 for the values and most of 1.8 for ACT. e9 also runs at full clock where the kernel before ran at half, so its 7.8 is not the forecast's sum borne out term by term.

**The rival that named the time** (the order gives the gain back, 1337.6) was right in size and wrong in mechanism: e1 and e7 keep the order and differ by 1.5% of the time. Lock stays and bank dearer fall by the groups above; slower didn't come: the reduces into the bank cost 7 ns each, not 200.

**Products free of POOL** (0.64): right. The 65 ns more for a PSUM source that the Trainium skill's page "VectorE: DVE Perf Modes", section on the TRN2 errata, led me to estimate don't show: 679 ns from the bank, where two SBUF operands take 707 to 880 in the groups of the runs. The Trainium skill has a rule that fits the second figure in "SBUF — State Buffer", "Who interferes with whom": a VectorE instruction with two SBUF inputs contends with a GpSimd instruction that reads SBUF. The trace agrees: of the products with two SBUF operands in the kernel before, those that run beside POOL's work take 0.94 (L2240) and 0.86 us (L2252) on average and the others 0.68; from the bank it is 0.68 in both cases. But what DVE saved was sized by occupation and not by path: of 8.3 us the bank gave 1.0 a turn and the norms nothing (72.9 against 73.0 in e13); DVE is idle for 11 us a turn in e1 (72.9 - 61.5). Of the 3 us from a clean old turn (75.9) to e1's, some 2 are left for the order. That is a subtraction and not shown: the order wasn't run by itself.

**New wait, norms.** DVE waits 5.1 us in five turns for the values (forecast: up to 1.3 each): right. DVE busy 61.5 (61 to 63): right. ACT's six norms take 0.60 to 0.62 us each, not "at most the 0.47" of a Gelu, which cost nothing beside ACT's 51 us of 76. The groups of POOL over the five turns of the changed kernel:

```profile
L1798 POOL TENSOR_TENSOR d_xstats<-d_xstats,mhalf 128x1 f32<-128x1 f32 x9 | 5.2, 577 | 0.0
...
L1802 POOL TENSOR_TENSOR d_ystats<-d_ystats 128x1 f32<-128x1 f32 x10 | 1.9, 193 | 1.4
```

Of the added [128x1] products only the negation for x3 takes the 0.55 that I took, the others 0.19 (the other end was nothing). So the last norm ends 1.83 us after the last variance (1331.30 to 1333.13), before 1.18 (1341.45 to 1342.63): 0.65 more, not 2.0.

**Experts** (3.6): 4.0 in the profile of the changed kernel, 1.6 in that of e8, 4.6 (2.3 to 6.9) by e8's runs (e2, whose experts are those of the kernel before, took 183.7 in its profile, 2.1 less than that kernel's, so single profiles differ by as much): right within that, but the wait before the fourth rows, "at most 1 us", is 1.8 and 2.6. **Next interval** (2.0): 2.3. **End** (2.0): 0.8.

## What to carry to other kernels

A timetable made of durations at full clock is a bound, not a forecast, where the change lengthens or gathers PE's waits: list the waits of the new order, and price behind each long one what the trace shows behind such waits now (here 1.9 us a turn in the kernel before, 3.3 for the two of a changed turn). PE's idle time was not free here even where the loop needs it; filled with matmuls that nobody reads it gave 21 us. And what an engine saves counts only along the chain that closes the loop.

## What the runs showed of the hardware that I had not expected

The clock fell to half in the midst of dense work, for some 3 to 7 us, in or just behind waits of 2.5 to 2.9 us, ten times of ten in the changed kernel. The length of a wait alone doesn't tell: waits of 2.5 were followed by a slow stretch in every turn of e7, beside others of 3.1, and in two turns of five in e3, where the other was filled; one of 2.12 in three of five in the kernel before; and three times, there and in e2, one of 1.3 was, where most waits of that length were not. The Trainium skill describes such a loop in "TensorE: Matmul & The Clock Gate", "HAM oscillation — how this bites in real kernels", for waits on DMA; the changed kernel's trace agrees that each turn pays anew (ten stretches of 1.2 GHz in five turns), while in e3 and in the kernel before not every turn does. GpSimd's product of two [128x1] operands takes 0.19 us in five of its six groups where the power of that shape takes 0.55.
